# A block pipeline on one core: the first half of the W_out product moved to the end of the iteration, with new orders on the other engines

## The reference

```
u = x @ W_in + b_in;  g = sigmoid(x @ W_gate + b_gate)
h_t = tanh(h_{t-1} @ A + u_t @ Bm)
y_t = h_t @ C.T + u_t @ D.T;   ys = g * y + (1 - g) * x
x1  = layernorm(x + (ys @ W_out + b_out + x))
out = layernorm(x1 + gelu(x1 @ bw1.T + b1) @ bw2.T + b2)     # bw: row scale times sign of w; 1024 hidden units
```

## Time and profile before

| | |
|---|---|
| runs, us | 447.81 (447.3 to 448.36) |
| profiled execution, us | 449.45 |
| its span, first to last instruction, us | 447.6 |
| PE busy | 426.4 us, 95% |
| DVE busy | 363.0 us, 81% |
| ACT busy | 309.5 us, 69% |
| POOL busy | 302.0 us, 67% |
| mean granted TensorE clock | 0.990 |

### The profile page before, as it was taken

One profiled execution on the slowest core, in us unless ns is written; L12 is line 12 of the kernel. 1 busy time (PEld: TensorE's weight loads), 2 busy tenths in 40 slices (PEclk: granted clock), 3 DMA queues, 4 the chain that ended last, 5 costly groups with the idle time before them and its releaser, 6 DMA issues.

```text
span 447.6 us, 8039 instructions
## 1 busy us (share of the span) xinstructions
PE 426.4 (95%) x2687; PEld 304.1 (68%) x2687; DVE 363.0 (81%) x791; ACT 309.5 (69%) x570; POOL 302.0 (67%) x302
## 2 busy tenths in 40 slices
PE   7999999999889989999999999999999999999882
PEld 4787877777445666777767767677686776766551
DVE  3666678744681889999999999999999999998584
ACT  1222224656335858798898988989889898797791
POOL 5199622332459597978879779797797977683523
PEclk9999999999998999999999999999999999999997
DMA  7944450000110103122241423413333133230222
GB/s 226 362 162 128 127 123 1 1 0 1 47 48 2 47 1 93 49 50 94 52 137 48 97 95 65 125 48 96 108 79 98 48 95 119 71 96 36 60 94 94
DMA packets 43893, 37.16 MB, mean 83 GB/s; under 512 B 35504, under 2 KB 37296, under 8 KB 43856
## 3 DMA queue, kind: packets, MB, share of 16 engines
q1 hardware_dynamic: 42528, 35.66, 27.6%
q0 software_dynamic: 272, 0.66, 0.5%
q10 hardware_dynamic: 1056, 0.36, 0.3%
HBM read 19.90 MB, written 8.39 MB: 63 GB/s over the span
## 4 chain that ended last, share of the span: by engine, by line
PE 64%; DVE 21%; issue 5%; ACT 4%; POOL 3%; DMA 1%; SPq 0%; DVEq 0%; POOLq 0%; ACTq 0%
PE bank L1006 15%; PE bank L994 12%; PE bank L968 9%; PE bank L860 7%; DVE hid L1304 7%; PE bank L772 7%; PE bank L765 6%; PE bank L757 3%; DVE bank L1287 3%; ACT hid L629 3%; DVE gT L1317 3%; PE bank L950 2%; DVE bank L1310 2%; DVE gT L1299 2%; PE bank L846 1%
## 5 line engine op out<-in xcount | busy, mean ns | idle before, releaser
L994 PE MATMUL bank<-xT,w1s 128*128 128x512 f16 x512 | 126.9, 380 | 2.8 <-DVE hid L1304 2.2
L1006 PE MATMUL bank<-w2s,hid 128*128 128x256 f16 x1024 | 125.4, 273 | 0.9 <-DVE gT L1317 0.8
L1006 PEld LDWEIGHTS bank<-w2s,hid 128*128 128x128 f16 x1024 | 98.6, 98 | 31.5 <-issue 5.6
L621 ACT ACTIVATE bank<-bank,b_col,alpha 128x512 f32<-128x512 f32 x128 | 96.7, 755 | 17.6 <-PE bank L994 17.2
L1304 DVE SCALAR_TENSOR_TENSOR hid<-bank,small,hid 128x512 f16<-128x512 f32 x128 | 94.8, 742 | 14.3 <-ACT hid L629 14.3
L629 ACT ACTIVATE hid<-bank,small 128x512 f16<-128x512 f32 x128 | 86.5, 691 | 19.1 <-PE bank L1006 18.0
L994 PEld LDWEIGHTS bank<-xT,w1s 128*128 128x128 f16 x512 | 46.0, 98 | 49.9 <-DVE hid L1304 7.4
L405 POOL TENSOR_TENSOR ys_lo<-gT,ys_hi 128x512 fp32r<-128x512 f32 x32 | 40.8, 1276 | 25.0 <-ACT ys_hi L596 24.9
L401 POOL TENSOR_TENSOR gT<-gT,xT 128x512 f32<-128x512 f32 x32 | 40.8, 1274 | 20.0 <-DVE gT L1259 19.5
L772 PE MATMUL bank<-hu,w_rec 128*128 128x128 f32 x208 | 45.5, 301 | 1.1 <-DVE hu L1117 0.9
L421 POOL TENSOR_TENSOR gT<-x_rows,b_row 128x1024 f32<-128x1024 f32 x16 | 38.0, 2377 | 7.8 <-DMA xT<-gT 7.7
(11 more groups left out here) (135 smaller groups left out, 807.3 us busy)
## 6 DMA issues: line engine op xcount, KB each, us to landing
x_load<-in_L_attn_x SPq DMA_DIRECT2D x16, 512.0 KB, 3.4
gT<-in_L_attn_x SPq DMA_DIRECT2D x15, 512.0 KB, 3.8
out_rows<-gT SPq DMA_DIRECT2D x15, 512.0 KB, 2.6
gT<-in_L_ffn_w SPq DMA_DIRECT2D x2, 1024.0 KB, 11.9
gT<-in_L_attn_x SPq DMA_DIRECT2D x4, 128.0 KB, 2.7
out_rows<-gT SPq DMA_DIRECT2D x2, 256.0 KB, 2.0
xT<-gT SPq DMA_TRANSPOSE x28, 3.2
w_gate<-in_L_attn_W_gate ACTq DMA_DIRECT2D x1, 256.0 KB, 7.0
```

The costliest lines, as they stand in the source:

```text
L621: nc.scalar.activation(bank[which][:, :], bank[which][:, :], ACT.Gelu, bias=b1_col[:, c:c + 1], scale=alpha1[:, c:c + 1]).then_inc(s_gelu, 1)
L994: done = nc.tensor.matmul(bank[which][:, :], w1s[:, c, k, :], x1T[:, n, :, part, :, k, :], start=(k == 0 and part == 0), stop=(k == KD - 1 ...
L1006: done = nc.tensor.matmul(bank[tile // 2][:, tile % 2 * DM:(tile % 2 + 1) * DM], hid[:, c % 3, part, tile * P:(tile + 1) * P], w2s[:, :, c ...
```

## The change

Only the five orders inside `iteration` change (four engines; SP's is the same). On PE out0 goes from between h6 and h7 to the end of the iteration, so that it stands directly ahead of the next iteration's y1 and out1; y0 goes ahead of h3; f2 ahead of h5, h6 ahead of f3, f4 ahead of h7. DVE takes `first_sum` first, the two `first_norm` later in part, and `second_moments` from the front to the middle; ACT takes `second_norm(n-3, 3)` from between two early chunks to behind `x1_copy(n+1, 0)`; POOL takes `hu_low` directly behind `residual`. What runs before and after the loop is unchanged. The same instructions are issued, as many as before.

```diff
@@ PE
                 if due(n):
                     hidden(n, 1)
                     hidden(n, 2)
-                    hidden(n, 3)
                 if due(n + 3):
                     y_products(n + 3, 0)
                 if due(n):
+                    hidden(n, 3)
                     ffn_out(n, 0)
                     hidden(n, 4)
                     ffn_out(n, 1)
+                    ffn_out(n, 2)
                     hidden(n, 5)
-                    ffn_out(n, 2)
+                    hidden(n, 6)
                     ffn_out(n, 3)
-                    hidden(n, 6)
+                    ffn_out(n, 4)
+                    hidden(n, 7)
                 if due(n + 2):
                     out_products(n + 2, 0)
-                if due(n):
-                    hidden(n, 7)
-                    ffn_out(n, 4)
@@ POOL
                 if due(n):
                     residual(n)
+                if due(n + 3):
+                    pool.wait_ge(s_x1b, n + 1)
+                    hu_low(n + 3, 0)
+                    hu_low(n + 3, 1)
                 if due(n + 1):
                     first_rstd(n + 1, 0)
-                if due(n + 3):
-                    pool.wait_ge(s_rs1, n * 2 + 3)
-                    hu_low(n + 3, 0)
-                    hu_low(n + 3, 1)
...
@@ ACT
+                if due(n + 1):
+                    x1_copy(n + 1, 0)
                 if due(n - 3):
                     second_norm(n - 3, 3)
...
@@ DVE
-                if due(n - 2):
-                    second_moments(n - 2)
                 if due(n + 1):
                     first_sum(n + 1, 0)
-                    first_spread(n + 1, 0)
...
```

More of the change, by code:

```diff
@@ L461, in iteration @@
                     ys_low(n + 2, 0)
+                    ys_low(n + 2, 1)
                 if due(n - 2):
@@ L464, in iteration @@
                 if due(n + 2):
-                    ys_low(n + 2, 1)
                     add_bias(n + 2)
@@ L640, in iteration @@
             def iteration(n):
-                if due(n - 3):
-                    second_norm(n - 3, 1)
                 if due(n - 1):
@@ L646, in iteration @@
                     hidden_gelu(n - 1, 7)
-                if due(n - 3):
-                    second_norm(n - 3, 2)
+                if due(n + 3):
+                    hu_high(n + 3, 0)
                 if due(n - 1):
                     hidden_hi(n - 1, 7)
+                if due(n - 3):
+                    second_norm(n - 3, 1)
                 if due(n + 3):
-                    hu_high(n + 3, 0)
                     hu_high(n + 3, 1)
@@ L655, in iteration @@
                     hidden_gelu(n, 0)
-                    hidden_hi(n, 0)
-                if due(n + 1):
-                    x1_hi(n + 1, 0)
                 if due(n + 2):
@@ L661, in iteration @@
                 if due(n):
+                    hidden_hi(n, 0)
+                if due(n - 3):
+                    second_norm(n - 3, 2)
+                if due(n):
                     hidden_gelu(n, 1)
+                    hidden_gelu(n, 2)
                     hidden_hi(n, 1)
-                    hidden_gelu(n, 2)
+                    hidden_hi(n, 2)
+                    hidden_gelu(n, 3)
+                if due(n + 2):
+                    ys_high(n + 2, 1)
+                if due(n):
+                    hidden_hi(n, 3)
+                if due(n + 1):
+                    x1_hi(n + 1, 0)
+                if due(n):
+                    hidden_gelu(n, 4)
+                if due(n + 1):
+                    x1_hi(n + 1, 1)
+                if due(n):
+                    hidden_hi(n, 4)
+                if due(n + 1):
+                    x1_copy(n + 1, 0)
                 if due(n - 3):
@@ L667, in iteration @@
                 if due(n):
[L668 to L671, removed]
-                if due(n):
[L673 to L680, removed]
                     hidden_gelu(n, 5)
-                    hidden_hi(n, 4)
-                    hidden_hi(n, 5)
+                if due(n - 2):
+                    second_norm(n - 2, 0)
                 if due(n + 1):
                     x1_copy(n + 1, 1)
-                if due(n - 2):
-                    second_norm(n - 2, 0)
+                if due(n):
+                    hidden_hi(n, 5)
             gate(GATED, 1)
@@ L1343, in iteration @@
                 if due(n + 1):
+                    first_spread(n + 1, 0)
+                    first_sum(n + 1, 1)
                     first_moments(n + 1, 0)
+                if due(n - 1):
+                    hidden_lo(n - 1, 7)
                 if due(n + 2):
                     less_x(n + 2, 1)
-                if due(n - 1):
-                    hidden_lo(n - 1, 7)
                 if due(n + 1):
-                    first_sum(n + 1, 1)
-                    first_norm(n + 1, 0)
                     first_spread(n + 1, 1)
@@ L1354, in iteration @@
                     gate_y(n + 2, 1)
-                if due(n + 1):
-                    first_moments(n + 1, 1)
                 if due(n):
@@ L1361, in iteration @@
                     ffn_scale(n - 1, 1)
+                if due(n + 1):
+                    first_moments(n + 1, 1)
+                if due(n - 1):
                     second_sum(n - 1, 0)
@@ L1366, in iteration @@
                 if due(n + 1):
-                    first_norm(n + 1, 1)
-                    x1_lo(n + 1, 0)
+                    first_norm(n + 1, 0)
                 if due(n):
@@ L1371, in iteration @@
                 if due(n + 1):
-                    x1_lo(n + 1, 1)
+                    first_norm(n + 1, 1)
+                if due(n - 2):
+                    second_moments(n - 2)
                 if due(n):
                     hidden_lo(n, 3)
[L1375 to L1380, removed]
+                if due(n + 1):
+                    x1_lo(n + 1, 0)
+                    x1_lo(n + 1, 1)
                 if due(n):
@@ L1383, in iteration @@
                 if due(n + 3):
+                    less_x(n + 3, 0)
                     gate_y(n + 3, 0)
+                if due(n - 1):
+                    second_spread(n - 1, 0)
                 if due(n):
                     hidden_lo(n, 5)
+                if due(n - 1):
+                    second_spread(n - 1, 1)
             def align(n):
```

## The result

The changed kernel takes 460.5 us (four runs, 458.0 to 463.21) against 447.65 (447.3 to 448.36) before: a ratio of 1.029, interval 1.023 to 1.035. Forecast were 449.2, with a range of 446.4 to 451.4. The profiled execution took 458.0, with a span of 456.2 at a mean clock of 0.995.

What follows compares the result with a forecast made beforehand. PE was taken to set the pace, busy 95% of the span. Span 447.6, less 0.1 up to block 15's h0, plus 1.5 clock loss, gave 449.0; +1.4 carried to the 447.81 median gave 449.2 us, range 446.4 to 451.4.

Steps and rivals of the forecast that it cites:

- Part 1: PE's out0 moved to other neighbours: still 12 matmuls, 1.44 us in either place, so an effect of 0.
- Part 2: Steady loop: reordered DVE cuts PE's wait from 0.22 to 0.06 us, period 18.41 to 18.25; 2.7 us gained by iteration 13.
- Part 3: SP's turns queue behind late norm and store; second lands F+14.95 (F: end of f6), h0 may start F+15.5 (15.0 to 15.9).
- the store's company: Delay of the turns by the 512 KB store in flight just ahead: 0 to 0.9 us, 0.5 taken.
- The cover: Steady-loop slack: h0 due at F+15.64, y0 at F+20.86 after POOL's residual and hu_low; 0.1 to 0.3 us.
- The upper bound: Most the store could delay the turns: 0.9 us, from the trace's slowest turn, 4.1 against 3.2.
- The rule on ring order: SP's first turn moves only after the store's data; upper half of 0 to 0.9 likelier, sum some 0.2 us worse.
- Part 4: Loop end: PE waits for turns until block 15's h0 at F+15.5, losing 2.2 us; 420.8 against 420.92, -0.1 so far.
- Part 5: PE's 3.4 us stand before block 15 drops the clock, about 3 us at half speed: 1.5 us lost (0 to 1.7).
- Rival 3: Store costs turns the full 0.9; h0 waits for the landing every iteration, period 18.5: 453.0 us, chance 0.14.
- rival 2: Store doesn't delay the turns, which land in 3.2; period 18.20, clock stays up in a 2.9 us gap: 446.2, chance 0.16.

Runs made afterwards that it cites:

- Experiment 7: Kernel before with only PE's iteration order of the changed kernel, the other engines in their old orders: 468.92 us, ratio 1.05.
- experiment 2: Changed kernel with ACT's second_norm(n-3, 3) moved early, right behind second_norm(n-3, 2): 444.78 us, ratio 0.9937 to the kernel before.
- experiment 4: Changed kernel with the two turns ahead of the store in SP's queue, ACT's norm kept late: 445.59 us, ratio 0.9958.
- experiment 9: Changed kernel with second_norm(n-3, 3) early and the warm-up as 38 matmuls of 80 columns: 445.31 us, ratio 0.9956.
- experiment 1: Changed kernel with the warm-up as 38 matmuls of 80 columns instead of 6 of 512, moving the instruction fetch earlier: 448.9 us, ratio 1.0044.
- experiment 3: Changed kernel without the 13 stores of the loop, their waits kept: 450.84 us, ratio 1.0102.
- Experiment 8: Changed kernel with the warm-up as 12 matmuls of 256 columns, 6 more, moving the fetch only slightly: 461.09 us, ratio 1.032.
- experiment 11: Kernel before with the warm-up as 38 matmuls of 80 columns and nothing else: 448.19 us, ratio 1.0.
- experiment 5: Kernel before with the warm-up as 16 matmuls of 192 columns instead of 6 of 512: 447.74 us, ratio 1.0007.

## Why the prediction was wrong

- **Part 1 (out0's own move 0): right**, on PE. Experiment 7 shows that the other engines' orders must move with it, by its trace DVE's `first_sum` above all.
- **Part 2 (period 18.25): right.** 18.18 to 18.20 while nothing holds the turns, about the same in experiments 2, 4 and 9, and 18.18 to 18.30 in experiment 1, where the turns just fit. The little gap ahead of h5 is gone.
- **Part 3 (the turns late): the step that failed.** "The second lands 3.2 later" with 0 to 0.9 for the store's company, 0.5 taken. The mechanism, the queue behind the late norm and its times were right, and the store's price too: in experiment 1 the turns are issued at 304.71 and POOL's residual starts at 309.89, 5.2 later, against 1.31 + 3.2 and 0.1 for the release, 4.6, without company. The store costs 0.6. What is missing is a term that nothing in the sum had: the fetch, 1.4 (308.58 to 315.15 is 6.6, less 5.2). So the turns' company costs 2.0 where 0.5 was taken and 0.9 was the bound. The cover bears 0.64 of company (15.64 less 15.0): the store alone just fits (experiment 1), the fetch alone passes it by some tenths (experiment 3), both pass it by 1.3. With it h0 comes at F+17.0, past the 15.64 at which it is due, so each of ten iterations is 1.3 longer. The upper bound was wrong in kind: the 4.1 from which the 0.9 came was itself a turn that met a small fetch (8 KB, at 251.48 in the list of packets, turns 250.10 to 253.29), not the worst case of a store. And the cover of "0.1 to 0.3" was called barely enough without asking what else is on the DMA engines at F+12 to F+16.
- **The rule on ring order** (the Trainium skill, "DMA: Bandwidth & Descriptors", section "Queues, rings and completion order": on each DMA engine descriptors are consumed in ring order) was weighed for the store alone. The trace agrees with it as far as the store goes: in experiment 1 the turns' first packet starts at 306.59, the store's last one ends at 306.85, and the price is 0.6, in the upper half. But the store was the wrong company to weigh alone.
- **Part 4 (block 15's h0 at F+15.5): right.** No fetch is there; it came at F+15.57, PE standing for 3.42. Length: forecast 0.1 less than before; experiment 1, which has all of the change but the collision, has 0.46 less.
- **Part 5 (the clock): right as a mechanism, wrong for the execution shown.** Windows of PE around the gap (window, length, PE busy, ..., granted clock, DMA share, GB/s), first in the changed kernel, then in experiment 1:

```profile
426.10:429.40 3.30, 0.00 (x0) 0.00 (x0) 2.88 (x9) 2.72 (x5) 0.00 (x0) 1.00 0.95 175
429.50:432.00 2.50, 2.50 (x16) 1.55 (x17) 0.17 (x1) 0.75 (x1) 2.45 (x2) 1.00 0.02 7
```

```profile
415.80:419.10 3.30, 0.00 (x0) 0.00 (x0) 2.89 (x9) 2.71 (x5) 0.00 (x0) 1.00 0.95 175
419.20:421.00 1.80, 1.80 (x8) 0.81 (x7) 0.16 (x1) 0.40 (x1) 1.80 (x1) 0.61 0.00 0
421.00:424.00 3.00, 3.00 (x16) 1.82 (x15) 0.00 (x0) 0.35 (x1) 2.73 (x7) 0.67 0.00 0
```

  It is the same gap of 3.4 us, and in one execution the clock stays up while in the other PE works at the lower level of 1.2 GHz in part of the next 5 us. The tail is 14.68 in the first and 16.36 in the second: 1.7 us, where 1.5 was taken and 1.7 was the bound. Experiment 8 lost the same 1.7 after 3.38, experiment 4 1.5 after 2.40; experiment 3 nothing after 2.41. The length of the gap alone doesn't tell which, so this term belongs in a sum with a weight. Only one execution of each kernel was profiled. The rule that the throttled state is the default and activity releases it (the Trainium skill, "TensorE: Matmul & The Clock Gate", section "What's actually happening") made the gap look dangerous; by these rows it is, in some executions and not in others.
- **The rivals.** Rival 3's outcome (h0 waits for the landing in every iteration) is what happened, in ten of fourteen iterations, but its cause, the store at its full 0.9, gives 453.0; the fetch was not among the causes, so no case reached 460. Turns that land in 3.2, rival 2's condition, are what experiments 2 and 4 made: 444.8 and 445.6 against its 446.2. But they also issue the turns 1.5 us earlier, which rival 2 didn't have, so they don't confirm its sum.

The sum again, in the profiled executions: experiment 1, all of the change without the collision, has a length of 257.07. The changed kernel has 269.71, 12.6 more. Its nine periods from y1 at 214.33 to y1 at 389.72 are 1.30 above 18.19 on the mean, and with the tenth late h0 that is 13.0; experiment 1's own periods there are 0.04 above 18.19, which takes off 0.4. Without the collision the whole loss is gone; what is left of the change without it, and with the norm early, is a gain of 2.6 us in length (257.53 to 254.89).

## What to carry to other kernels

When a change makes a DMA late, list everything else that uses the DMA engines where it will now be, instruction fetches (a queue of their own in the profile) included, and price the cover against their sum. By experiment 1 this fetch follows TensorE's own count of instructions, so it could be shifted past a sensitive transfer by 32 matmuls ahead of the loop (the 6 of experiment 8 were too few); the sturdier repair is to give the transfer its cover back, here by one instruction of ScalarE. And ask of every engine, not only of the one at the end of the chain, who waits for a landing and what is queued behind that wait.

## What was not expected of the hardware

- In the changed kernel one packet of 16 KB in the instruction queue (0.9 to 1.0 us long) holds 16 to 21 packets of 256 bytes of two transposing DMAs for 1.2 to 2.1 us, and the landing goes from 3.2 to between 4.6 and 5.6. In eight of its ten collisions the last packet of the turns started 2.2 us after the fetch. Why these packets wait longer than the fetch takes isn't settled.
- A fetch that came up to 2.1 us after the start of the two turns' data (2.75 us long when nothing disturbs it), or just ahead of it, broke in (experiments 3, 8 and 11, and the changed kernel); in experiment 5 and in half of the iterations before, it started within 0.15 us of their last packet. That it is kept back when it falls due late in the data is a guess; no run here varied that alone.
- A store of 512 KB issued directly ahead of the two transposing DMAs makes their issues take 3.06 in place of 2.61 and their landing 3.5 in place of 3.2. Issued directly behind them it takes 0.58 to issue in place of 0.34 and costs them nothing.
- With the same gap of 3.4 us on TensorE ahead of block 15's h0, the granted clock fell in two profiled executions of three (experiments 1 and 8; not in the changed kernel).
